# A rotary table built in four parts, and a softmax whose subtraction and exponentials go by score bank

## What is computed

```python
for i in range(DEPTH):                       # 6
    x = attn_layer(shift_tokens(x), Wqkv[i], q_scale[i], k_scale[i], Wo[i]) + x
    x = ffn_layer(shift_tokens(x), ln_g[i], ln_b[i], W1[i], b1[i], W2[i], b2[i]) + x
# attn_layer: 16 heads of 64
q = l2norm(q) * qs;  k = l2norm(k) * ksc
q = q * cos * scale + rotate_half(q) * sin * scale
k = k * cos * inv + rotate_half(k) * sin * inv
# windows of 32 queries against 64 keys (their own window and the one before), masked
sim = einsum('bhwie,bhwje->bhwij', bq, bk2) * 8
attn = softmax(where(mask, -max, sim), -1)
```

## Time and profile before

| | |
|---|---|
| time, median of 3 runs (lowest to highest) | 4713.65 us (4701.56 to 4717.32) |
| profiled execution: its own time, and its span | 4716.82 us, 4715.0 us |
| PE, matmul, busy | 4152.8 us (88%) |
| DVE busy | 2916.5 us (62%) |
| ACT busy | 2620.6 us (56%) |
| POOL busy | 2778.1 us (59%) |
| mean granted clock of TensorE | 0.955 |
| step of the local layers, p = 0 to 1, to 2, to 3 | 36.7 to 36.8 us |

### The profile page before, as it was taken

How to read it: one execution, slowest core, us unless ns; L and a number is a source line. 1 busy time by engine, 2 the same in 40 slices (tenths; PEclk the granted TensorE clock), 3 DMA queues, 4 the chain that set the end, 5 groups by cost and what they waited for, 6 DMA issues and landing times. The chain is left out here.

```text
span 4715.0 us, 163424 instructions
## 1 busy us (share of the span) xinstructions
PE 4152.8 (88%) x67078; PEld 2779.2 (59%) x67078; DVE 2916.5 (62%) x4217; ACT 2620.6 (56%) x4417; POOL 2778.1 (59%) x3434
## 2 busy tenths in 40 slices
PE   5878788689999999999999999999999999999994
PEld 2434344356666666666666666666666666666663
DVE  5565656466666666666666666666666666666664
ACT  2535354446556555665556565655666556665562
POOL 0000000177777777777777777777777777777771
PEclk8989798889999999999999999999999999999997
DMA  0000000112222222222222222222222222222222
GB/s 27 3 15 2 16 10 8 42 45 56 65 69 67 59 68 71 69 56 67 65 69 64 56 65 69 66 56 65 78 68 54 68 67 69 64 56 65 69 71 74
DMA packets 284548, 258.85 MB, mean 55 GB/s; under 512 B 122872, under 2 KB 258509, under 8 KB 271149
## 3 DMA queue, kind: packets, MB, share of 16 engines
q1 hardware_dynamic: 283820, 248.14, 19.7%
HBM read 117.63 MB, written 29.77 MB: 31 GB/s over the span
## 5 line engine op out<-in xcount | busy, mean ns | idle before, releaser
L785 DVE TENSOR_TENSOR products<-bank_d,table 128x1024 f32<-128x1024 f32 x772 | 937.9, 1215 | 711.9 <-ACT sq L612 696.2
L905 POOL TENSOR_TENSOR products<-products 128x2048 f32<-128x2048 f32 x192 | 870.9, 4536 | 282.9 <-DVE products L785 282.7
L411 PE MATMUL bank_d<-w_qkv,xT 128*128 128x512 f32 x1544 | 807.6, 626 | 21.5 <-DVE products L785 10.4
L612 ACT ACTIVATE sq<-bank_d 128x512 f32<-128x512 f32 x772 | 468.0, 606 | 482.9 <-PE bank_d L411 472.7
L942 POOL TENSOR_TENSOR qk_rot<-products,rnorm 128x2048 f32<-128x2048 f32 x192 | 695.4, 3622 | 14.9 <-POOL rnorm L924 14.6
L783 DVE TENSOR_REDUCE ss<-sq 128x16 f32<-128x1024 f32 x386 | 468.6, 1214 | 235.8 <-ACT sq L612 235.8
L949 POOL TENSOR_TENSOR prob<-prob,inv_sum 128x1024 f32<-128x1024 f32 x192 | 365.1, 1902 | 406.1 <-DVE inv_sum L765 406.1
L872 POOL MEMSET ident<- 128x128 f32 x1 | 0.2, 204 | 920.4 <-POOLq L1060 920.4
L1487 DVE TENSOR_REDUCE part_max<-s_max 128x1 f32<-128x512 f32 (+3 forms) x768 | 399.0, 554 | 152.6 <-PE s_max L1236 101.9
L457 PE MATMUL bank_a<-ident,qk_rot 128*128 128x128 f32 x3072 | 412.0, 290 | 70.5 <-issue 37.4
L457 PEld LDWEIGHTS bank_a<-ident,qk_rot 128*128 128x128 f32 x3072 | 366.4, 149 | 152.7 <-issue 105.1
(11 more groups left out here) (168 smaller groups left out, 7536.1 us busy)
## 6 DMA issues: line engine op xcount, KB each, us to landing
v_back<-v SPq DMA_DIRECT2D x96, 768.0 KB, 5.6
w_qkv<-in_Wqkv_dram SPq DMA_DIRECT2D x25, 1024.0 KB, 5.1
v_back<-v SPq DMA_DIRECT2D x192, 128.0 KB, 5.5
w_qkv<-in_Wqkv_dram SPq DMA_DIRECT2D x25, 512.0 KB, 5.4
xs<-x_layers SPq DMA_DIRECT2D x194, 64.0 KB, 2.1
w_o<-in_Wo_dram SPq DMA_DIRECT2D x24, 512.0 KB, 5.2
xr<-x_layers SPq DMA_DIRECT2D x96, 128.0 KB, 2.2
x<-x SPq DMA_DIRECT2D x96, 128.0 KB, 1.8
```

What stands on the lines that cost most here:

```text
L411: nc.tensor.matmul(bank[:, :], xT[:, P * a:P * (a + 1)], w_qkv[:, col:col + 512], start=True, stop=True).then_inc(d_filled if i < 8 else a ...
L612: nc.scalar.activation(sq[j % 2][:, 8 * c:8 * c + 8, :], bank_d[slot][:, :].rearrange("p (h d) -> p h d", d=DH), ACT.Square).then_inc(squa ...
L785: nc.vector.tensor_tensor(products[:, a, head:head + 8, :, :].rearrange("p h r (o d) -> p h r o d", o=2), bank[:, :].rearrange("p (h r d) ...
L905: link(nc.gpsimd.tensor_tensor(products[:, a, :, 0, :], products[:, a, :, 0, :], products[:, a, :, 1, :], ALU.add))
```

## The change

The table is written by `make_table(f, p)` in four parts of two token tiles, two operations of 128x256 elements each. The part for the next round's pair p stands at the end of step p, behind `norm_qk` of tile 1, in place of the whole table in step 3. `table_ready` counts parts; DVE waits for the part of its pair at chunk 0 of every pair, SP for four parts.

`softmax_shift` subtracts with two operations of 128x512, one for each score bank, each of which raises `scores_used`. `exponentials` runs two activations of 128x512, each behind its half of the subtraction; `exp_done` is raised by the second. On PE each bank of `score` waits for its own half of the previous subtraction. The maximum, the sum and POOL's normalisation stay whole.

```diff
--- before.py
+++ after.py
@@ -329,7 +329,7 @@
                     sp.dma_start(xr[back2.par][:, :, :], dram_rows(x_dram, back2.f, 1 + PAIR * back2.p, PAIR)
                                  .rearrange("(a t) d -> t a d", a=2)).then_inc(xr_in[back2.par], 16)
                 if runs(now) and s.p == 0:
-                    sp.wait_ge(table_ready, s.f + 1)
+                    sp.wait_ge(table_ready, POS * (s.f + 1))
                     load_qk_rows(s.f + 1)
                 if runs(now) and s.p == POS - 1:
                     sp.wait_ge(d_filled, chunk_at(now, 7)[1] + 1)
@@ -460,9 +460,9 @@
             def score(s, pair, ph, half):
                 if half == 0:
                     pe.wait_ge(a_free, ring_a.at(s, "qk7")[1] + 1)
-                    n = 2 * pair.n + ph
-                    if later(n):
-                        pe.wait_ge(scores_used, n)
+                n = 2 * pair.n + ph
+                if later(n):
+                    pe.wait_ge(scores_used, 2 * (n - 1) + half + 1)
                 first = pair.p == 0 and ph == 0
                 bank = scores[:, 4 * half:4 * half + 4, :, :]
                 nc.tensor.matmul(bank, ident_b[:, :], mask[:, int(first), :, :, :], start=True, stop=False,
@@ -644,8 +644,11 @@
                 nc.scalar.activation(out, bank, ACT.Copy).then_inc(a_free, 1)
 
             def exponentials(pair, ph):
-                act.wait_ge(scores_used, 2 * pair.n + ph + 1)
-                nc.scalar.activation(prob[ph][:, :, :], prob[ph][:, :, :], ACT.Exp).then_inc(exp_done, 1)
+                for half in range(2):
+                    hu = slice(HEADS // 2 * half, HEADS // 2 * (half + 1))
+                    act.wait_ge(scores_used, 2 * (2 * pair.n + ph) + half + 1)
+                    ins = nc.scalar.activation(prob[ph][:, hu, :], prob[ph][:, hu, :], ACT.Exp)
+                ins.then_inc(exp_done, 1)
 
             def copy_probs(s, ph):
                 for half in range(2):
@@ -752,9 +755,11 @@
                 if later(n, 2):
 
                     dve.wait_ge(a_filled, ring_a.at(prev(s), f"PT{2 * ph + 1}")[1] + 1)
-                nc.vector.tensor_tensor(prob[ph][:, :, :], sc,
-                                        row_max[:, ph, :].unsqueeze(2).to_broadcast([P, HEADS, 2 * WINDOW]),
-                                        ALU.subtract).then_inc(scores_used, 1)
+                for half in range(2):
+                    hu = slice(HEADS // 2 * half, HEADS // 2 * (half + 1))
+                    nc.vector.tensor_tensor(prob[ph][:, hu, :], sc[:, hu, :],
+                                            row_max[:, ph, hu].unsqueeze(2).to_broadcast([P, HEADS // 2, 2 * WINDOW]),
+                                            ALU.subtract).then_inc(scores_used, 1)
 
             def softmax_sum(s, ph):
                 if not runs(s.pair(1)):
@@ -770,8 +775,8 @@
                 if not runs(pair):
                     return
                 a, kind, c = chunks[i]
-                if i == 0 and pair.p == 0:
-                    dve.wait_ge(table_ready, pair.f + 1)
+                if i == 0:
+                    dve.wait_ge(table_ready, pair.n + 1)
                 slot, n = chunk_at(pair, i)
                 bank = bank_d[slot]
                 t4 = table[:, 2 * pair.p + a, :, :, :]
@@ -889,18 +894,21 @@
                 nc.gpsimd.memset(mask[32 * q:32 * q + 32, 1, :, 0, 0:WINDOW], MASKED).then_inc(constants_ready, 1)
             pool.wait_ge(constants_ready, INIT)
 
-            def make_table(f):
+            def make_table(f, p):
+
                 pool.wait_ge(qkrow_in, 16 * (f + 1))
+                rows = slice(2 * p, 2 * p + 2)
                 for sin, quarters in ((0, slice(0, 4, 3)), (1, slice(2, 0, -1))):
                     ins = nc.gpsimd.tensor_tensor(
-                        table[:, :, :, quarters, :],
-                        rotary[:, :, sin::2, :].rearrange("p t k (o d) -> p t k o d", o=2),
+                        table[:, rows, :, quarters, :],
+                        rotary[:, rows, sin::2, :].rearrange("p t k (o d) -> p t k o d", o=2),
                         qk_row[:, sin::2, :].rearrange("p k (o d) -> p k o d", o=2).unsqueeze(1)
-                        .to_broadcast([P, SEQ // P, 2, 2, DH // 2]), ALU.mult)
+                        .to_broadcast([P, 2, 2, 2, DH // 2]), ALU.mult)
                 ins.then_inc(table_ready, 1)
 
             pool.wait_ge(rotary_in, 16)
-            make_table(0)
+            for p in range(POS):
+                make_table(0, p)
             def add_products(s, a):
                 link(nc.gpsimd.tensor_tensor(products[:, a, :, 0, :], products[:, a, :, 0, :], products[:, a, :, 1, :], ALU.add))
 
@@ -966,11 +974,10 @@
                     normalise(back1, 1)
                 if runs(now):
                     pool.wait_ge(d_free, chunk_at(now, 7)[1] + 1)
-                    if s.p == POS - 1:
-                        make_table(s.f + 1)
                     add_products(s, 1)
                     inverse_norms(1)
                     norm_qk(s, 1)
+                    make_table(s.f + 1, s.p)
                 if s.p == POS - 1:
                     nc.gpsimd.sem_clear(p_link)
                     links[0] = 0
```

## The result

The changed kernel takes 4775.91 us (median of 4 runs, 4757.21 to 4787.63) against 4710.41 us for the kernel before beside it. The ratio is 1.0134, 95% interval 1.0109 to 1.0158. The forecast was 4685 us, in a range of 4668 to 4708; it was wrong in sign.

The account below looks back on a forecast made before the run. PE was taken to set the pace, held up by ACT's `yT` and gelu. Gains of 1.2 + 1.1 + 21.6 + 3.5 + 1.0 = 28.4 us off 4713.65 gave 4685 us, range 4668 to 4708.

Parts of the forecast that it names:

- The table: POOL's table in four parts: gains 0 us at the 22 turns, parts of 1.45 us hidden in POOL's idle time.
- The two names of the stall: PE's waits on `qk_rot` at the turn (33.2 us in 11) taken as the same stall that sits at the loop's branch.
- The 42.17 us: Length read for the step across the loop's turn, 5.45 us more than an undisturbed step.
- The 2.3 us at the two ends: Table in parts: first rotations earlier at the loop's start, 1.2 us; PE's `qk_rot` wait after the loop, 1.1 us.
- The chain: Softmax on ACT and DVE, through `yT` and table load to gelu, delays PE; halves gain 0.36 us in 60 steps, 21.6 us.
- the 36.3 to 36.4: Sign of being right: steps p = 0 to 3 of the changed kernel last this many us.
- the other terms: Gains besides the 60 steps: 1.2 and 1.1 us (table), 3.5 (35 steps), 1.0 (step after the loop).
- the disturbed steps: Some 35 steps where PE comes late after a stall at or behind a turn: 0.1 us each, 3.5 us.
- the rival of full lengths: Softmax halves do not overlap, each pays its full length: 0.17 us a step, about 4700 us; chance 0.17.
- PE's new waits: Loop-counter waits at each second score bank, 192 times: the change loses above 0.15 us each; nothing expected to show.
- the turns unchanged at about 42 us: Sign of being right: turns keep this length, with 2.5 to 3.3 us idle ahead of tile 0.
- the one that ends slower: Handling PE's counter-dependent waits costs more than the change saves; 4735 us at 0.25 us each; chance 0.09.

Follow-up runs that it names:

- N = 256: Kernel before with 256 more satisfied waits ahead of PE's loop, executed once: 4961.46 us, ratio 1.0565.
- the 36 waits: Kernel before with 36 satisfied waits at the very end of PE's loop body: 4785.43 us, ratio 1.0162.
- N = 128: Kernel before with 128 more satisfied waits ahead of PE's loop, executed once: 5002.62 us, ratio 1.0623.

## Why the prediction was wrong

**The table: right.** The turn's excess was PE's own stall and not POOL's table; the table alone gives 1.0003. The two names of the stall are one thing, as I took it: in the trace of before the stalls at the turn that are named after `qk_rot` end 1.6 to 1.8 us behind a code packet, as those named "issue" do. The 42.17 us, though, were misread as the step across the turn. That stretch begins at 2616.20 us, behind nearly all of the idle 2.66 us; by PE's first transposes the excess lies in two steps, 40.25 and 38.63 us. In the second PE is busy 1.8 us longer than in the undisturbed one, at a clock of 0.96, and it has the `xn` stall. The parts cost 1.42 us (1.45 forecast) in an idle time that covers them. The 2.3 us at the two ends are too small to be told by the medians. In the traces the way from the first transpose of the local layers to the first of step 4 is 1081.29 - 934.03 = 147.3 us before and 1075.49 - 929.69 = 145.8 with the table alone, against 1.2 forecast for the start.

**The chain: mechanism right, size somewhat high.** Subtraction to `yT` is 1.86 us, where the sum had 1.83: 0.36 less than before. The exponentials of phase 0 cost 1.15 against 1.06 us, so 0.09 and not 0.03. The net is 0.27 us a step and not 0.36, and the steps agree: p = 1 and 2 go from 36.83 and 36.80 to 36.59 and 36.54 us with PE's program untouched, so they did not reach the 36.3 to 36.4 that I had named as a sign. 60 x 0.27 = 16 us would come from the steps, where I had 21.6, and with the other terms as forecast the sum would be 23 us. The whole change with PE's program untouched gives 0.38% of 4701.54, 17.9 us (10.8 to 24.9), of 28.4 forecast; no run tells the terms for the disturbed steps and the ends apart. The time alone would also fit the rival of full lengths, some 13 us, but the rows don't: two exponentials take 1.15 us and not 1.19, two subtractions 1.29 and not 1.38. The rule of the Trainium skill on the fixed cost of an instruction (VectorE: DVE Perf Modes, section on the TRN2 errata), by which a split would cost an estimated 0.19 us on ACT and 0.13 on DVE, is too high here: 0.09 and 0.07 (1.29 against 1.22) were measured.

**PE's new waits: this step failed.** I priced them as handling, 0.15 us each from which the change would lose, and put them near zero because a wait behind a whole bank of scores leaves no gap in the rows. That reading held: where no stall falls, step p = 1 is 36.62 us with them. And a constant wait costs 0.055 us even where nothing hides it, 11 us for 192 of them (the new ones have threshold arithmetic besides). But handling was the wrong price. The waits add 36 instructions to the loop and 5 ahead of it, and so they move all code behind them and lengthen the loop. The stalls marked "issue", which the profile of before showed at the turn and which I took as fixed ("the turns unchanged at about 42 us"), move with the code, because PE stands still until a code packet has come. In the changed kernel one lands in the score products of step p = 2 (36.80 to 38.04 us) and one just ahead of the turn (41.01 to 42.96), while the one at `xn` in step p = 0 is gone. A round goes from 153.2 to 156.4 us, which over 22 rounds makes the 71 us between the two profiled executions. PE's waits alone cost 2.19%; the halves give back 0.24 to 0.38% of it, and the third stall of that kernel, in step p = 1, 0.96 us on average in each of 22 rounds, is absent from most rounds of the changed kernel. PE's program is the same in both, so the place is not all that decides; I don't know what else does.

**Of the rivals** the one that ends slower was right about the edit and wrong about the mechanism; its last sentence, that PE's queue could run dry, is what happened, at a chance that was too low.

**What stays open.** Why the times return at 512 and not at 256, though a packet holds about 256 instructions (512 are two packets), and by what rule a place stalls or not. The runs show that the place matters and that a stall ends when a code packet has come, not how to compute which packet is late. A 23rd packet in the round goes with a loss in three kernels, but N = 256 loses 260 us with 22. How much of the 36 waits' 76 us at the turn is their own time is open too.

## What to carry to other kernels

On an engine that is the bound and whose code runs in a long unrolled loop, count the instructions that an edit adds to it, register arithmetic for thresholds included, before believing any saving below 1%: here 36 instructions cost 1.3 to 2.2%. Make the handshake fit the busy engine's old program (a second semaphore between the other two engines here) and the edit can be judged by itself. When "issue" stalls appear in a dense stretch, compare their ends with the packets of the instruction queue, and shift the code with idle instructions ahead of the loop and time it: that separates the edit from its place. Price the idle instructions by a second count of them.

## What the runs showed of the hardware

The same loop, instruction for instruction, took 153.2, 153.3, 154.3, 163.3 or 166.4 us a round as it stood 0, 512, 5, 256 or 128 instructions further on: up to 9% of a round, and 6% of the kernel. That is far more than anything the change was about.

PE's code came in packets of 16,384 bytes, 22 or 23 a round, each under way for about 1.1 us. PE's stalls without a releaser ended 1.1 to 1.9 us behind the end of such a packet, in 754 of 764 cases. Most were 1 to 5 us long. In dense stretches of score products (32 in 1.1 us) PE stopped for about 1.2 us, and at the turn of the loop for 2.9 us, or 5 to 6 us with N = 128 and with the 36 waits at its end.

Behind the longer stalls the granted clock was lower (0.56 of full speed behind one of 2.41 us), and with N = 256 PE's own work took 92 of the 221 us that 22 rounds lost. A satisfied wait on PE's queue cost 0.055 us where PE had nothing else to do.
